# The second mixture of experts: seven single blocks spread between pair blocks

## The chip, the cores and the metric

The kernel runs on one core of a Trainium2 chip. The metric is the device time of one execution in microseconds (us). Below, TensorE is the matrix engine (PE in the profile), VectorE is DVE, ScalarE is ACT, GpSimd is POOL and SyncE is SP; SP only issues transfers here, and POOL issues the gathers and scatters by index.

## The reference

Two layers run one after the other over x of 4 x 1024 tokens with 256 numbers each. Each is x + mixer(norm(x)) * silu(ffn(norm(x))). The change touches only the expert part of the second layer:

```
gate_scores = jax.nn.softmax(x @ Wg + bg, axis=-1)
topk_scores, topk_idx = jax.lax.top_k(gate_scores, TOP_K)      # 2 of 8 experts
...
for e in range(NUM_EXPERTS):
    h = jax.nn.gelu(x @ W1[e] + b1[e])                         # 256 -> 1024
    y = h @ W2[e] + b2[e]                                      # 1024 -> 256
    output = output + y * combine_w[..., e:e + 1]
```

4096 tokens choose two experts each, so 8192 rows go through an expert. With the inputs used here the eight experts are chosen 1101, 1114, 920, 949, 1048, 972, 1104 and 984 times.

## The kernel before

The rows of the second expert part are gathered into blocks, and every block belongs to one expert. A **pair block** holds 256 rows (two tiles of 128), a **single block** holds 128. There are 32 pair blocks and 7 single blocks, 71 tiles in all. The routing on VectorE works out at run time which expert a block belongs to (`slot_expert`), which tokens its tiles gather (`token_of`) and to which rows of `result1` its output is scattered (`result_of`). With the counts above all 32 pair blocks hold rows, four of them in each expert, and four of the seven single blocks do; the last three single blocks are empty, and their scatters point past the end of the result and write nothing.

For the n-th block in order of processing (n from 0 to 38) the engines do this:

- SP loads the whole expert, 2180 KB, into one of three buffers, `WE[n % 3]` (line 2143). It may do so when block n-3 has left `WE`, that is when VectorE has taken the output of n-3 out of its bank (line 2142).
- POOL gathers the block's tiles into `xg` (line 1988, one indirect transfer for each tile).
- TensorE turns the rows (line 1078, "xg_turn"), multiplies them by W1 in eight column groups (line 1092, 32 matmul records of 256 columns for a pair block, 32 of 128 columns for a single one), and multiplies the result by W2 (line 1102, 32 records for a pair block, 16 for a single one). ScalarE copies the turned rows (line 1889) and does the gelu of each column group (line 1902). VectorE adds the bias and takes the output out of its bank (line 1651).
- POOL scatters the output, one indirect transfer for each tile (line 1999).

The order is written out once for all engines by `schedule1` (each engine walks the same list and does its own part). This is the loop, with the parts for the attention of layer 1 left out:

```
    for n in range(NSLOT):
        if n + 2 < NSLOT:
            add("load_rows1", n + 2)
        add("w1", n)
        if n + 1 < NSLOT:
            add("xg_turn", n + 1)
...
        add("w2", n)
...
        add("y1_out", n)
        if n + WR < NSLOT:
            add("load_weights", n + WR)
        if n == XS_AT:
            add("load_xs")
```

`WR` is 3 and `XS_AT` is 19. `load_xs` is 16 transfers of 512 KB each on SP (lines 2117 and 2118) that bring `x1` and the attention output `s1` back from memory for the final mix. They stand in SP's list behind the weights of block 22 and ahead of the weights of block 23, and SP issues in order. After the last block SP waits for all scatters and issues 16 loads of the results (line 2155, `both`); the final mix on ScalarE and VectorE and the stores (line 2158) follow.

`SLOT_TILES` gives each block's number of tiles in order of processing, and `SLOT_AT` its first tile in `token_of` and `result_of`. Before, `SLOT_TILES` is 32 twos and then 7 ones.

Of the kernel before, what the change touches and what calls it, by code (L numbers as in the profile page):

```python
# [24 lines left out]

E1, F1, TOPK = 8, 1024, 2
PAIR_SLOTS, SINGLE_SLOTS = T * TOPK // (2 * P), E1 - 1
SLOT_TILES = [2] * PAIR_SLOTS + [1] * SINGLE_SLOTS
SLOT_AT = [sum(SLOT_TILES[:n]) for n in range(len(SLOT_TILES))]
NSLOT = len(SLOT_TILES)  # L30
TILES1 = sum(SLOT_TILES)
SLOTS1 = TILES1 * P
# [10 lines left out]
def constants():  # L43
# [12 lines left out]
        ("row_no", np.tile(np.arange(P), (P, 1))),  # L56
        ("slot_start", np.tile(np.array(SLOT_AT) * P, (P, 1))),
    ]
# [440 lines left out]
def build(nc, a, out):  # L499
# [314 lines left out]
    def tensor(e):  # L814
        w = Waits(e)

        def fill_from(u):
            w.wait_ge(free[u.bank], u.before)

        def emptied(item):  # L820
            w.wait_ge(free[use[item].bank], use[item].emptied)
# [209 lines left out]
        for what, *at in plan1:  # L1031
# [38 lines left out]
            elif what == "xg_turn":  # L1070
                n, = at
                u = use["xg_turn", n]
                w.wait_ge(xg_in[n % XR], 16 * sum(SLOT_TILES[n % XR:n + 1:XR]))
                fill_from(u)
                out_v = PS[:, u.bank, :].rearrange("p (k n) -> p k n", k=KD)
                for j in range(SLOT_TILES[n]):
                    for k in range(KD):
                        m = e.transpose(out_v[:, k, j * P:(j + 1) * P], xg[:, n % XR, j, k * P:(k + 1) * P], ident)
                m.then_inc(full[u.bank], 1)
            elif what == "w1":  # L1080
                n, = at
                rows = SLOT_TILES[n] * P
                emptied(("xg_turn", n))
# [839 lines left out]
    def gpsimd(e):  # L1923
# [47 lines left out]
        for what, *at in plan1:  # L1971
# [6 lines left out]
            elif what == "load_rows1":  # L1978
# [7 lines left out]
                for j in range(SLOT_TILES[n]):  # L1986
                    tile = SLOT_AT[n] + j
                    e.indirect_dma_start(  # L1988
# [3 lines left out]
            elif what == "y1_out":  # L1992
# [4 lines left out]
                for j in range(SLOT_TILES[n]):  # L1997
                    tile = SLOT_AT[n] + j
                    e.indirect_dma_start(  # L1999
# [205 lines left out]
```

## Time and profile before

| | |
|---|---|
| median of 3 runs | 1260.48 us (1258.74 to 1261.28) |
| the profiled execution | 1254.79 us, of which span 1253.0 us |
| TensorE busy | 1097.0 us, 88% |
| VectorE, ScalarE, GpSimd busy | 52%, 43%, 29% |
| mean granted TensorE clock | 0.911 of full speed |
| expert blocks of layer 1 | 622 to 1205 us of the span |
| final mix and stores | 1208 to 1253 us |

Times inside the trace count from the start of the span. The profiled execution is 1.79 us longer than its span, and the median of the runs is 5.69 us above it. Busy shares are averages over stages with different limits; which engine sets the time of one stage is read from the waits in that stage.

### The profile page before, as it was taken

To read this page: it belongs to the slowest core of one execution; us is meant where nothing else is said; L and a number is where in the kernel's file an instruction comes from. 1 tells how busy PE (TensorE), PEld (TensorE's weight loads), DVE (VectorE), ACT (ScalarE), POOL (GpSimd) and SP (SyncE) were. 2 spreads that over 40 slices of the span, in tenths; PEclk is the share of its full clock that TensorE was granted. 3 is DMA by queue.
4 is the path that set the end of the run, shared out by engine and by line. 5 is a ranking of instruction groups with operands and counts; after the bars stand their busy time and mean duration, and the time that the engine had idled before them with its cause. 6 is when DMAs were issued, how large, how long until landed. Compare 5 with 4: busy or idle time off the path is not lost.

```text
span 1253.0 us, 16201 instructions
## 1 busy us (share of the span) xinstructions
PE 1097.0 (88%) x6006; PEld 958.5 (76%) x6006; DVE 645.6 (52%) x1330; ACT 539.3 (43%) x1133; POOL 368.1 (29%) x351
## 2 busy tenths in 40 slices
PE   3955699999999994999698999999999999999940
PEld 2933578888888883888587888888888888888940
DVE  6384477667677775646697656564710000000018
ACT  2212355455454445565545454554323332233445
POOL 1007144444444541000314323232223322222200
PEclk9677699999999997787598999999999999999975
DMA  9802402443343335426146434343555895455948
GB/s 294 239 8 102 151 1 84 133 127 100 113 126 119 113 113 182 166 83 256 72 152 244 148 143 156 134 170 118 194 191 193 288 395 185 177 185 198 337 154 269
DMA packets 100624, 207.07 MB, mean 165 GB/s; under 512 B 9819, under 2 KB 86119, under 8 KB 95553
## 3 DMA queue, kind: packets, MB, share of 16 engines
q1 hardware_dynamic: 88976, 174.70, 40.1%
q0 software_dynamic: 11568, 31.34, 7.6%
q8 instruction: 48, 0.79, 0.3%
q14 instruction: 32, 0.25, 0.1%
HBM read 159.08 MB, written 48.97 MB: 166 GB/s over the span
## 4 chain that ended last, share of the span: by engine, by line
PE 73%; DMA 5%; ACT 5%; issue 3%; SPq 3%; DVE 3%; POOL 1%; POOLq 0%; ACTq 0%
PE PS L1102 17%; PE PS L1092 16%; PE PS L843 7%; PE PS L994 5%; PE PS L933 4%; PE PS L882 4%; PE PS L1004 2%; PE PS L946 2%; PE PS L960 2%; PE PS L1054 2%; PE PS L891 2%; PE PS L971 2%; PE PS L832 1%; SPq L2117 1%; PE PS L1067 1%
## 5 line engine op out<-in xcount | busy, mean ns | idle before, releaser
L1092 PE MATMUL PS<-xgT,WE 128*128 128x256 f32 (+1 forms) x1248 | 259.6, 366 | 12.8 <-ACT xgT L1889 6.2
L1902 ACT ACTIVATE hT<-PS,WE 128x256 f32<-128x256 f32 (+1 forms) x312 | 139.9, 454 | 281.0 <-PE PS L1092 271.6
L1092 PEld LDWEIGHTS PS<-xgT,WE 128*128 128x128 f32 x1248 | 222.2, 193 | 43.5 <-ACT hT L1902 8.5
L1102 PE MATMUL PS<-WE,hT 128*128 128x256 f32 x1136 | 251.6, 379 | 0.0
L1102 PEld LDWEIGHTS PS<-WE,hT 128*128 128x128 f32 x1136 | 213.5, 190 | 27.8
L1651 DVE TENSOR_TENSOR y<-PS,WE 128x512 f32<-128x512 f32 (+1 forms) x39 | 25.1, 643 | 365.5 <-PE PS L1102 365.5
L1999 POOL DMA_INDIRECT result<-y,result_of x71 | 71.3, 1004 | 277.3 <-DVE y L1651 267.2
L1988 POOL DMA_INDIRECT xg<-xn_dram,token_of x71 | 73.6, 1037 | 152.8 <-DVE result_of L1567 131.4
L843 PE MATMUL PS<-XT,Wf 128*128 128x256 f32 x384 | 91.6, 397 | 0.0
L843 PEld LDWEIGHTS PS<-XT,Wf 128*128 128x128 f32 x384 | 76.4, 203 | 10.6
L1957 POOL TENSOR_TENSOR prob<-prob,row_sum 128x512 f32<-128x512 f32 x56 | 58.6, 1046 | 73.8 <-DVE row_sum L1307 73.4
L1950 POOL TENSOR_TENSOR sc<-sc,sc_max 128x512 f32<-128x512 f32 x56 | 58.4, 1043 | 71.8 <-DVE sc_max L1295 70.9
L933 PE MATMUL PS<-KB,Q 128*128 128x256 f32 x256 | 71.0, 403 | 7.2 <-DVE KB L1269 5.8
L994 PE MATMUL PS<-rowsT,wgu 128*128 128x160 f32 x512 | 75.6, 301 | 0.0
L994 PEld LDWEIGHTS PS<-rowsT,wgu 128*128 128x128 f32 x512 | 72.4, 190 | 2.6 <-issue 1.4
L832 PE MATMUL PS<-const,XN 128*128 128x128 f32 x128 | 32.0, 410 | 39.4 <-ACT XN L1840 19.2
L1976 POOL TENSOR_TENSOR MAG<-SQ 128x768 f32<-128x768 f32 x16 | 28.9, 1811 | 123.5 <-ACT SQ L1862 123.5
L882 PE MATMUL PS<-XT,qkv_w 128*128 128x256 f32 x256 | 63.0, 392 | 0.0
L832 PEld LDWEIGHTS PS<-const,XN 128*128 128x128 f32 x128 | 22.2, 206 | 46.8 <-ACT XN L1840 24.0
L1305 DVE TENSOR_REDUCE row_sum<-prob 128x8 f32<-128x512 f32 x64 | 43.6, 681 | 27.8 <-ACT prob L1781 23.7
L933 PEld LDWEIGHTS PS<-KB,Q 128*128 128x128 f32 x256 | 46.5, 202 | 13.4 <-DVE KB L1269 6.9
L882 PEld LDWEIGHTS PS<-XT,qkv_w 128*128 128x128 f32 x256 | 50.9, 199 | 7.5
(227 smaller groups left out, 1690.8 us busy)
## 6 DMA issues: line engine op xcount, KB each, us to landing
WE<-in_experts SPq DMA_DIRECT2D x39, 2180.0 KB
wgu<-in_w_gate SPq DMA_DIRECT2D x32, 256.0 KB, 2.7
wgu<-in_w_up SPq DMA_DIRECT2D x32, 256.0 KB, 3.1
wdn<-in_w_down SPq DMA_DIRECT2D x32, 256.0 KB, 3.4
both<-result SPq DMA_DIRECT2D x16, 512.0 KB, 8.7
table<-zeros POOLq DMA_DIRECT2D x1, 5160.0 KB, 29.5
rows<-table SPq DMA_DIRECT2D x32, 129.0 KB
X<-in_x SPq DMA_DIRECT2D x8, 512.0 KB, 9.5
```

The costliest lines, as they stand in the source:

```text
L832: m = e.transpose(out_v[:, k, j * P:(j + 1) * P], XN[:, 2 * pair + j, k * P:(k + 1) * P], ident)
L843: m = e.matmul(PS[:, u.bank, part * CH:(part + 1) * CH], Wf[:, n, k, part * P:(part + 1) * P], XT1[:, ch, k, :], start=k == 0, stop=k == K ...
L882: m = e.matmul(PS[:, u.bank, c * UT:(c + 1) * UT], qkv_w[:, k, col:col + P], XT0[:, unit, k, :], start=k == 0, stop=k == KD - 1)
L933: m = e.matmul(PS[:, u.bank, c * 256:(c + 1) * 256], Q2[:, unit % 2, c, win, :, :].rearrange("p e q -> p (e q)"), KB[:, c, win, :, :].rear ...
L994: m = e.matmul(PS[:, u.bank + f, n * CAP:(n + 1) * CAP], wgu0[:, ex % 2, n, k, f * P:(f + 1) * P], rowsT[:, grp % 2, k, j * CAP:(j + 1) * ...
L1092: m = e.matmul(PS[:, FIRST_H_BANK + nth % HR, 0:rows], W1[n % WR][:, k, c * P:(c + 1) * P], xgT[:, n % 2, k, 0:rows], start=k == 0, stop=k ...
L1102: m = e.matmul(PS[:, u.bank, j * D:(j + 1) * D], hT[:, n % 2, c, j * P:(j + 1) * P], W2[n % WR][:, c, :], start=c == 0, stop=c == KF - 1)
L1902: e.activation(hT[:, n % 2, c, 0:rows], PS[:, FIRST_H_BANK + (KF * n + c) % HR, 0:rows], ACT.Gelu_apprx_tanh, bias=b1[n % WR][:, c:c + 1], ...
L1950: e.tensor_tensor(by_head, by_head, sc_max[:, s % SR, :].unsqueeze(2).to_broadcast([P, PAIRS, WIN]), ALU.subtract).then_inc(sc_sub_done, 1)
L1957: e.tensor_tensor(prob[:, s % PR0, :, :], prob[:, s % PR0, :, :], row_sum[:, s % RR, :].unsqueeze(2).to_broadcast([P, PAIRS, WIN]), ALU.mu ...
L1988: e.indirect_dma_start(out=xg[:, n % XR, j, :], out_offset=None, in_=xn_dram, in_offset=bass.IndirectOffsetOnAxis(ap=token_of[:, tile:tile ...
L1999: e.indirect_dma_start(out=result1, out_offset=bass.IndirectOffsetOnAxis(ap=result_of[:, tile:tile + 1], axis=0), in_=y1[:, n % YR, j, :], ...
```

## The change

The seven single blocks no longer stand at the end of the list. The first is put at index 18, behind 18 pair blocks, and the others at 20, 22 and so on to 30, so that one pair block stands between two single ones. Eight pair blocks (31 to 38) follow the last single block. Each block keeps its tiles, its tokens and its expert; only the place in the order moves. Nothing is added or removed.

```
-SLOT_TILES = [2] * PAIR_SLOTS + [1] * SINGLE_SLOTS
-SLOT_AT = [sum(SLOT_TILES[:n]) for n in range(len(SLOT_TILES))]
+FIRST_SINGLE = 18
+BLOCKS = [(2, 2 * n) for n in range(PAIR_SLOTS)]
+for n in range(SINGLE_SLOTS):
+    BLOCKS.insert(FIRST_SINGLE + 2 * n, (1, 2 * PAIR_SLOTS + n))
+SLOT_TILES = [tiles for tiles, _ in BLOCKS]
+SLOT_AT = [at for _, at in BLOCKS]
```

Line numbers of the changed kernel are 4 higher. The first place is TensorE from the W2 product of block 19 to the W1 product of block 23. A row with `WE,hT` is W2, a row with `xgT,WE` is W1, a row with `const,xg` turns the rows of the next block. Before, all are pair blocks:

```order
L1102 MATMUL PS<-WE,hT 128x256 x16
L1092 MATMUL PS<-xgT,WE 128x256 x16
L1078 MATMUL PS<-const,xg 128x128 x4
L1102 MATMUL PS<-WE,hT 128x256 x16
L1092 MATMUL PS<-xgT,WE 128x256 x16
L1078 MATMUL PS<-const,xg 128x128 x4
L1102 MATMUL PS<-WE,hT 128x256 x16
L1092 MATMUL PS<-xgT,WE 128x256 x16
L1078 MATMUL PS<-const,xg 128x128 x4
L1102 MATMUL PS<-WE,hT 128x256 x16
L1092 MATMUL PS<-xgT,WE 128x256 x16
```

Now, at the same place of TensorE's list:

```order
L1106 MATMUL PS<-WE,hT 128x256 x16
L1096 MATMUL PS<-xgT,WE 128x128 x16
L1082 MATMUL PS<-const,xg 128x128 x4
L1106 MATMUL PS<-WE,hT 128x256 x8
L1096 MATMUL PS<-xgT,WE 128x256 x16
L1082 MATMUL PS<-const,xg 128x128 x2
L1106 MATMUL PS<-WE,hT 128x256 x16
L1096 MATMUL PS<-xgT,WE 128x128 x16
L1082 MATMUL PS<-const,xg 128x128 x4
L1106 MATMUL PS<-WE,hT 128x256 x8
L1096 MATMUL PS<-xgT,WE 128x256 x16
```

Blocks 20 and 22 have become single ones: W1 with 128 columns, and half as many W2 products. SP's list is the same in both kernels. This is its piece with the end of `load_xs` and the weights of block 23 (the changed kernel's lines):

```order
L2121 DMA xs_170<-x_dram 128x4x256
L2122 DMA xs_170<-s_dram 128x4x256
L2121 DMA xs_171<-x_dram 128x4x256
L2122 DMA xs_171<-s_dram 128x4x256
L2146 TENSOR_LOAD slot_expert
L2146 ISA x2
L2147 ISA
L2147 DMA WE<-in_experts 128x4360
```

Nothing moved there, so the sixteen `xs` transfers now stand beside smaller blocks. The third place is the end of POOL's list, where `result` rows are scatters and `xg` rows gathers. Before:

```order
L1999 DMA result<-y_163,result_of 8192x256
L1988 DMA xg<-xn_dram,token_of 128x256
L1999 DMA result<-y_163,result_of 8192x256
L1988 DMA xg<-xn_dram,token_of 128x256
L1999 DMA result<-y_163,result_of 8192x256 x3
```

Now:

```order
L2003 DMA result<-y_163,result_of 8192x256 x2
L1992 DMA xg<-xn_dram,token_of 128x256 x2
L2003 DMA result<-y_163,result_of 8192x256 x2
L1992 DMA xg<-xn_dram,token_of 128x256 x2
L2003 DMA result<-y_163,result_of 8192x256 x6
```

The last three blocks scatter two tiles each where they scattered one.

## Rows read from the trace of the kernel before

**Rows 1.** The page: the span, and busy time of the engines.

```profile
span 1253.0 us, 16201 instructions
PE 1097.0 (88%) x6006; PEld 958.5 (76%) x6006; DVE 645.6 (52%) x1330; ACT 539.3 (43%) x1133; POOL 368.1 (29%) x351
```

**Rows 2.** Chain that ended last, 974 to 1032 us: start, us, what.

```profile
974.13 6.92 PE PS L1102 x32
...
984.00 3.51 SPq L2117
...
1009.38 1.32 SPq L2118
...
1011.46 13.30 DMA WE<-in_experts
...
1024.89 7.14 PE PS L1092 x32
```

**Rows 3.** Timeline of PE, W1 of blocks 19, 20 and 23.

```profile
966.62 7.07 PE L1092 MATMUL PS<-xgT,WE 128*128 128x256 f32 x32
...
980.87 7.07 PE L1092 MATMUL PS<-xgT,WE 128*128 128x256 f32 x32
...
1024.89 5.42 PE L1092 MATMUL PS<-xgT,WE 128*128 128x256 f32 x24 [1.10 <-DMA WE<-in_experts]
```

**Rows 4.** Windows: busy by engine, granted clock, DMA share, GB/s at the end.

```profile
981.00:995.00 14.00, 14.00 (x69) 12.33 (x68) 0.69 (x1) 4.34 (x9) 4.05 (x4) 1.00 0.83 297
995.00:1009.00 14.00, 14.00 (x69) 12.32 (x68) 0.69 (x1) 4.35 (x9) 4.05 (x4) 1.00 1.09 354
1009.00:1024.00 15.00, 14.79 (x71) 12.69 (x69) 0.86 (x2) 4.34 (x9) 4.05 (x4) 1.00 1.08 395
...
1160.00:1168.00 8.00, 7.68 (x52) 7.05 (x52) 0.42 (x1) 3.32 (x9) 2.03 (x2) 1.00 0.94 353
...
1039.00:1053.00 14.00, 14.00 (x68) 12.34 (x67) 0.69 (x1) 4.35 (x9) 4.07 (x4) 1.00 0.52 193
```

**Rows 5.** DMA view of 1010 to 1015 us, then of 1020 to 1025 us.

```profile
DMA packets 1762, 1.74 MB, mean 349 GB/s; under 512 B 59, under 2 KB 1762, under 8 KB 1762
...
DMA packets 204, 2.12 MB, mean 424 GB/s; under 512 B 48, under 2 KB 48, under 8 KB 93
```

**Rows 6.** Timeline of the single blocks, 1160 to 1191 us.

```profile
1160.27 3.73 PE L1092 MATMUL PS<-xgT,WE 128*128 128x128 f32 x32
...
1162.97 1.03 POOL L1988 DMA_INDIRECT xg<-xn_dram,token_of  x1 [0.30 <-issue]
...
1171.87 0.20 PEld L1078 LDWEIGHTS PS<-const,xg 128*128 128x128 f32 x2 [0.28 <-DMA xg<-xn_dram,token_of]
...
1182.85 3.73 PE L1092 MATMUL PS<-xgT,WE 128*128 128x128 f32 x32
...
1190.10 3.73 PE L1092 MATMUL PS<-xgT,WE 128*128 128x128 f32 x32
```

**Rows 7.** PE behind two long waits (timeline), and a window behind the second.

```profile
622.27 10.07 PE L1092 MATMUL PS<-xgT,WE 128*128 128x256 f32 x32 [6.18 <-ACT xgT L1889]
...
678.32 6.77 PE L1092 MATMUL PS<-xgT,WE 128*128 128x256 f32 x20 [4.40 <-ACT hT L1902]
...
680.00:685.00 5.00, 5.00 (x18) 4.07 (x18) 4.93 (x10) 1.89 (x4) 0.80 (x1) 0.72 0.84 347
```

**Rows 8.** Timeline: output of a pair block, and of the last single one.

```profile
1153.22 0.69 DVE L1651 TENSOR_TENSOR y<-PS,WE 128x512 f32<-128x512 f32 x1 [13.34 <-PE PS L1102]
...
1155.99 0.97 POOL L1999 DMA_INDIRECT result<-y,result_of  x1 [0.30 <-issue]
...
1204.57 0.42 DVE L1651 TENSOR_TENSOR y<-PS,WE 128x256 f32<-128x256 f32 x1 [6.60 <-PE PS L1102]
```

**Rows 9.** Chain that ended last: last scatter of layer 0, last of layer 1.

```profile
478.37 2.17 DMA mixed_dram<-y,row_token
...
1205.77 2.10 DMA result<-y,result_of
```

## Prediction

> **What bounds the kernel now.** I read the page first. TensorE is busy 88% of a span of 1253.0 us [rows 1], so a change that moves only the order of its work matters where TensorE waits. Then I read the chain of waits over the expert blocks of the second layer. It is TensorE work almost without a break, with one exception: between 974 and 1025 us it leaves TensorE and runs through SP's issue of the `xs` transfers and then through the weights of block 23 [rows 2]. The reader should see three things there. The first `xs` transfers are issued at about 983 us and the last at 1009.38. The weights of block 23 (issued at 1011.46, landing 13.30 us later at 1024.76) come behind them. TensorE then waits for them, but only for 1.10 us [rows 3].
>
> The windows say why it is that long. From 981 to 1024 us the transfer engines are at shares of 0.83, 1.09 and 1.08, that is full, with 297, 354 and 395 GB/s, against 0.52 in the stretch of pair blocks behind it [rows 4]. The DMA view shows in what order the bytes move: from 1010 to 1015 us all 1762 packets are under 2 KB (the `xs` rows of 1 KB), from 1020 to 1025 us only 48 of 204 are [rows 5], the rest being expert weights. So the weights, issued at 1011.46, move behind the `xs` bytes and not beside them. This is a queue served in order, and the landing of block 23 is set by bytes and not by TensorE.
>
> The single blocks at the end, at a DMA share of 0.94 [rows 4], are near the transfer limit as well, but wait little. From W1 to W1 a single block takes 1190.10 - 1182.85 = 7.25 us; the three from 1160.27 to 1182.85 take 22.58, which is 0.83 above three times 7.25 [rows 6]. That 0.83 is late gathers.
>
> **The change part by part.** Sizes first. A pair block takes 980.87 - 966.62 = 14.25 us [rows 3], a single one 7.25 us [rows 6]. The number of both is unchanged, so the pure TensorE time is unchanged, and so is that of ScalarE, which does the gelu under it. What is left are waits.
>
> *The wait for the weights of block 23.* Call t0 the moment at which W2 of block 19 is done, 974.13 + 6.92 = 981.05 [rows 2]. Block 23's weights land at t0 + 43.7 and its W1 starts at t0 + 43.84 [rows 2]. Before, three pair blocks (20, 21, 22) stand between, 3 x 14.25 = 42.75, so the wait is 1.1. Now these are single, pair, single: 7.25 + 14.25 + 7.25 = 28.75. Does the landing come earlier with them? Its time is made of bytes: the weights of blocks 22 and 23 (2 x 2180 KB), 16 x 512 KB of `xs`, and the gathers and scatters of tiles of 128 KB. Before, three blocks bring 4 tiles each, so 12. Now the list gives scatter 19 (2 tiles), gather 22 (1), scatter 20 (1), gather 23 (2), scatter 21 (2), gather 24 (1), scatter 22 (1), gather 25 (2): again 12. The weights of block 22 are issued at t0 as before, the `xs` right behind; the weights of blocks 24 and 25 stand behind 23 in the queue. So I take the landing as unmoved, and the new wait is 43.84 - 28.75 = 15.1, which is **14.0 more than the 1.1 that it replaces**. Nothing hides it: the only later work that TensorE has is behind it in its own list. It would need a cover of 15 us, and both other buffers of `WE` have been used up. (The start of this stretch comes 7.0 earlier, block 18 being single, and behind it three more pair blocks and three fewer single ones are left, 3 x 7.0 = 21.0; the difference is the same 14.0.)
>
> The bounds of this term: all together are 12.85 MB and 12 x 0.131 MB, 14.4 MB, moved in about 42.4 us, 340 GB/s. At the 424 GB/s of the large packets [rows 5] they would take 34.0 us and the wait would be 6.7; at the 297 of the first window [rows 4], 48.5 and a wait of 21.2. I take the measured stretch itself, since the same bytes in the same order make it.
>
> The Trainium skill, "DMA: Bandwidth & Descriptors", section "Bandwidth", gives 425 GB/s for one 16 MB transfer into SBUF. By that figure the sum would be an estimate of some 9 us slower in place of the one below. The trace reaches it only with large packets; in the `xs` part it is 349.
>
> *Later weights.* Behind the wait, SP has already issued blocks 24 and 25 (their buffers are free from block 22's end at the latest), so they land under block 23. From then on single and pair alternate: a load is issued when block n is out and is needed two blocks later, 21.5 us. The run of single blocks shows loads that have only 14.5 us and cause no wait for `WE`. I cost this at nothing; the cover is one pair block, and without it the room is that of the single run.
>
> *The gathers.* The 0.83 us of late gathers goes away if a pair block lies between: **-0.83**. In the tightest new place, block 20, the gather of block 22 is issued some 4.3 us after W1 of block 20 begins and is needed 7.25 + 7.07 = 14.3 us after it. A gather issued at 1162.97 is waited for until 1171.87, 8.9 us at a DMA share of 0.94 [rows 6]. That leaves 1.1 us. At block 20 a miss costs nothing, the 15 us wait swallows it. At the five later places of this kind it would cost; I take 0, with a high end of 1 us each, 5.
>
> *The clock.* A wait of 15 us is new for TensorE in this stretch, where it has been granted 1.00. The two rows behind long waits show what comes next: after 6.18 us, the 32 records of W1 took 10.07 where they take 7.07, and after 4.40 us, 20 took 6.77 where they take 20/32 of 7.07, 4.4; in that stretch the granted clock is 0.72, a mix of the levels 1.2 and 2.4 GHz [rows 3, 7]. The costs are 3.0 and 2.4. I take the middle, **+2.7**; the low end is nothing (after the 1.1 us wait nothing was lost), the high end 3.0.
>
> *The end.* The last block is a pair block. VectorE's last step takes 0.69 in place of 0.42, and there is a second scatter, 0.97 + 0.30 [rows 8]: +1.54. The last scatter was of an empty block and ended 2.10 after its start; a scatter with rows, at the end of layer 0, took 2.17 [rows 9]. Together **+1.6**. The low end is 0.3, if the second scatter costs nothing; the high end puts the 8.9 of the loaded gather in place of 2.1, +8.4, which I think far off, since no weights move then.
>
> **Sum:** 14.0 - 0.8 + 2.7 + 1.6 = **+17.5 us**. Against the profiled execution, 1254.79, that is 1272.3; the median of the runs shown is 5.69 above that execution, so I forecast 1260.48 + 17.5 = **1278.0 us**.
>
> **The rivals.** *(A)* The forecast: the queue in order behind `xs`. For it: the 13.30 in the chain and the two kinds of packets [rows 2, 5]. Against: nothing in the trace; only the size is open.
>
> *(B)* Block 23's weights land in time. That needs them within 28.75 us of t0, so 14.4 MB at above 500 GB/s, or their passing the `xs` bytes. If it did, what remains is -0.8 + 1.6 = +0.8, at 1261.3, no difference. Against it: SP's issue itself is held until t0 + 30 by a full queue, its steps taking 1.32 to 3.51 us [rows 2].
>
> *(C)* The other side: the run of single blocks is transfer bound in the timed runs. Its share is 0.94 in the profile [rows 4], and the timed runs are 5.69 us longer than it. If all of that were weights arriving late in the run of single blocks, then spreading them gives it back: -5.7 - 0.8 + 1.6 = -4.9, at 1255.6. This decides only if B holds too, that is if the wait at block 23 stays under 5 us. Nothing in the profile shows a late `WE` in that run. The Trainium skill, "Perfetto Trace Analysis", section "Optimization Strategy", speaks for it: it says that regimes with different limits may gain from being interleaved, which is just what transfer-heavy single blocks among TensorE-bound pair blocks are. The trace gives this rule 0.83 us to win.
>
> *(D)* A, and the alternation brings late gathers in each single block: +5 on top, 1283.
>
> **How the numbers follow.** A has 80%, with a range of 1269 to 1285 (the wait between 6.7 and 21, drawn in towards the measured 15, and 2 us for the run-to-run spread of the medians); D has 9%, B 6%, C 5%. B and C together are 11%, so the range may leave them out and reaches into D: 1267 to 1286. A difference under 0.2% (2.5 us) can't be told from none. Faster by more: C, 5%. Within: B, 6%. Slower: A and D, 89%.
>
> **What would show it.** In the changed kernel's profile: one wait of TensorE at line 1096 for `WE` of 13 to 17 us, at about 1002 to 1018 us of the span, where the chain runs through SP's lines 2121 and 2122 and the weights; a granted clock under 1.00 in the 5 us behind it; no wait of TensorE for gathers between later single blocks, nor for weights; last scatter to first `both` load about the same, with the expert blocks ending 13 to 17 us later. The forecast is wrong if the weights of block 23 land earlier than t0 + 38 or the transfers' rate there differs by more than a tenth, if waits for `xg` appear in each single block, or if the last scatters take much longer than 2 us.

## The result and the profile after

The changed kernel takes 1275.58 us (median of 4 runs, 1272.84 to 1278.81) against 1260.88 us before (4 runs): a ratio of 1.012 with a 95% interval of 1.0092 to 1.0147, 14.7 us slower. The forecast was 1278.0 us, with a range of 1267 to 1286. Measured again on another chip, where both kernels are faster, it is 1245.41 against 1229.51, 1.0127 with an interval of 1.0103 to 1.0151, 15.9 us slower. Its profiled execution is 1275.98 us with a span of 1274.2 us, 21.2 us above the span of before.

First the page of the changed kernel: the span, and the slices of TensorE and of the granted clock.

```profile
span 1274.2 us, 16201 instructions
...
PE   4954699999999994999698999999999599999940
...
PEclk9667699999999996786598999999999889999975
```

There is one new hole in PE, the 5 in slice 32 (987 to 1019 us, 31.9 us a slice), and the clock's digits there and in the next slice are 8 where slices of full work have 9. The timeline of TensorE shows what it is, W1 of blocks 18, 20, 22 and 23:

```profile
954.98 3.73 PE L1096 MATMUL PS<-xgT,WE 128*128 128x128 f32 x32
...
976.48 3.73 PE L1096 MATMUL PS<-xgT,WE 128*128 128x128 f32 x32
...
997.98 3.73 PE L1096 MATMUL PS<-xgT,WE 128*128 128x128 f32 x32
...
1021.61 9.81 PE L1096 MATMUL PS<-xgT,WE 128*128 128x256 f32 x32 [16.01 <-DMA WE<-in_experts]
```

The last row answers to that of block 23 in [rows 3]: the wait for the expert's weights has gone from 1.10 to 16.01 us, and the 32 matmul records behind it take 9.81 us in place of 7.07. It is the only wait of TensorE between block 18 and the end; the kernel before had this one at 1.10 us and two of 0.3 us ahead of turns of gathered rows (at 1164 and 1171 us). The chain of waits takes the same way as before through SP [rows 2]:

```profile
969.73 6.92 PE PS L1106 x32
...
979.61 4.04 SPq L2121
...
1005.83 1.71 SPq L2122
...
1008.29 13.18 DMA WE<-in_experts
...
1021.61 9.81 PE PS L1096 x32
```

W2 of block 19 ends at 976.65. SP's issue of the `xs` transfers ends at 1007.5, 30.9 us later (29.7 before), the weights of block 23 move for 13.18 us (13.30), and W1 of block 23 begins 44.96 us after W2 of block 19 ended (43.84 before). The transfers kept their time to about 1 us, and TensorE came early. The windows of the changed kernel, with the granted clock third from the end, show the transfers full and the clock falling and coming back:

```profile
1001.65:1006.65 5.00, 3.95 (x21) 3.19 (x19) 0.42 (x1) 0.98 (x3) 1.36 (x2) 1.00 1.08 361
1006.65:1011.65 5.00, 0.00 (x0) 0.00 (x0) 0.00 (x0) 0.00 (x0) 3.04 (x3) 0.83 1.10 354
1011.65:1016.65 5.00, 0.00 (x0) 0.00 (x0) 0.00 (x0) 0.00 (x0) 0.00 (x0) 0.50 1.10 414
...
1021.65:1026.65 5.00, 5.00 (x12) 4.01 (x13) 0.00 (x0) 0.95 (x2) 0.00 (x0) 0.50 1.00 426
1026.65:1031.65 5.00, 5.00 (x24) 4.35 (x24) 0.00 (x0) 2.56 (x6) 0.00 (x0) 0.96 0.54 230
```

And the end, from the chain of the changed kernel, which answers to [rows 8, 9]:

```profile
1217.17 6.92 PE PS L1106 x32
1224.12 0.70 DVE y L1655
...
1225.59 0.97 POOL result L2003
1226.86 2.29 DMA result<-y,result_of
```

**Where the spans differ.** 21.2 us is more than the runs show, and part of it is not the change's. Block 18 is the first at which the kernels differ, and its W1 begins at 952.37 before and at 954.98 now, 2.6 later. From there to the end of the span it is 1253.0 - 952.37 = 300.6 us before and 1274.2 - 954.98 = 319.2 now, **18.6 us more**. I use this stretch for all traces below, since it leaves out what executions scatter ahead of block 18.

### The profile page after: what moved, and what is told of

It reads as the page before. It is cut to its first block, busy times and chain, and to the rows that moved or that the text cites. A ratio compares the mean times of both kernels' runs of the same rounds, so it can differ in the third digit from the quotient of the medians.

```text
span 1274.2 us, 16201 instructions
## 1 busy us (share of the span) xinstructions
PE 1100.7 (86%) x6006; PEld 963.4 (76%) x6006; DVE 645.4 (51%) x1330; ACT 539.0 (42%) x1133; POOL 368.0 (29%) x351
## 4 chain that ended last, share of the span: by engine, by line
PE 73%; ACT 5%; DMA 4%; DVE 3%; SPq 3%; issue 3%; another core or an unknown queue 2%; POOL 1%; POOLq 0%; ACTq 0%
PE PS L1106 18%; PE PS L1096 17%; PE PS L847 7%; PE PS L998 6%; PE PS L937 4%; PE PS L886 3%; PE PS L1008 2%; PE PS L964 2%; PE PS L1058 2%; PE PS L950 2%; PE PS L975 2%; PE PS L895 2%; PE PS L836 1%; SPq L2121 1%
## 5 line engine op out<-in xcount | busy, mean ns | idle before, releaser
L1096 PE MATMUL PS<-xgT,WE 128*128 128x256 f32 (+1 forms) x1248 | 262.3, 369 | 27.6 <-DMA WE<-in_experts 16.0
L836 PE MATMUL PS<-const,XN 128*128 128x128 f32 x128 | 31.9, 412 | 38.2 <-ACT XN L1844 18.9
L1980 POOL TENSOR_TENSOR MAG<-SQ 128x768 f32<-128x768 f32 x16 | 28.9, 1810 | 123.1 <-ACT SQ L1866 123.1
L950 PE MATMUL PS<-const,prob 128*128 128x128 f32 x256 | 40.9, 284 | 18.0 <-DVE prob L1314 10.0
```

Source lines behind the costliest of these rows:

```text
L836: m = e.transpose(out_v[:, k, j * P:(j + 1) * P], XN[:, 2 * pair + j, k * P:(k + 1) * P], ident)
L950: m = e.transpose(PS[:, u.bank, i * P:(i + 1) * P], prob[:, step % PR0, 2 * i:2 * i + 2, :].rearrange("p g k -> p (g k)"), ident)
L1096: m = e.matmul(PS[:, FIRST_H_BANK + nth % HR, 0:rows], W1[n % WR][:, k, c * P:(c + 1) * P], xgT[:, n % 2, k, 0:rows], start=k == 0, stop=k ...
```

## The experiments

The theory is that of the prediction: SP's queue is served in order, 8.4 MB of `xs` stand ahead of the weights of block 23, and single blocks give less TensorE work to cover them; the half-rate clock behind the wait and the second scatter at the end add to it. The rivals are that alternation costs by itself, that late gathers do, or that the wait is a matter of something else than bytes. In the edits shown, `...` marks lines left out. None of the kernels below leaves out work of the reference, and `filled` adds some that nobody reads.

**Stretch from W1 of block 18 to the end of the span, in us**

| kernel | W1 of 18 begins | span | stretch | expected | longest wait for WE |
|---|---|---|---|---|---|
| before | 952.37 | 1253.0 | 300.6 | | 1.1 |
| before, second profile | 958.37 | 1259.1 | 300.7 | 300.6 | 1.5 |
| changed | 954.98 | 1274.2 | 319.2 | | 16.0 |
| changed, second profile | 926.10 | 1245.3 | 319.2 | 319.2 | 16.2 |
| xs_last | 959.32 | 1259.6 | 300.3 | | none |
| singles_24 | 959.17 | 1260.2 | 301.0 | | 0.9 |
| old_xs31 | 957.71 | 1279.5 | 321.8 | | 19.1 |
| filled | 950.39 | 1266.6 | 316.2 | 316.3 | 1.2 behind 14.8 of work |
| xs_half | 950.40 | 1253.5 | 303.1 | 304 to 307 | 2.8 |
| empty_end | 948.59 | 1265.8 | 317.2 | 317.5 | 16.0 |
| covered | 948.85 | 1247.2 | 298.4 | 298.7 | none |
| covered, second profile | 927.52 | 1226.0 | 298.5 | 298.4 | none |

**xs_last: the new order, with the xs transfers behind all weights.**

```
-XS_AT = CHUNKS + 3
+XS_AT = NSLOT - 3
```

> The changed order, with load_xs moved from behind block 19 to behind block 36, where no weights are left to load. Theory A (the weights of block 23 queue behind the xs transfers): the 16.0 us wait of TensorE for WE is gone, the half-rate start behind it (2.9 us) too; the expert blocks end 18 to 19 us earlier than in the changed kernel, and two pair blocks (28.5 us) cover the xs transfers, so about 1258 to 1262 us, no difference from the kernel before (0.8 us of late gathers saved, 1.7 lost on the last scatters, 1.1 of the old wait saved). Rival 1 (alternating sizes or pair blocks at the end cost by themselves): most of the 15 us stays, over 1268. Rival 2: the xs transfers now delay the loads of the results, some 5 to 10 us come back, 1265 to 1270.

Measured: 1256.5 against 1258.0 us, ratio 0.9993 (0.9975 to 1.0011). TensorE does not wait once from block 18 on. Moving one entry of the list takes back 18.9 us, all of the 18.6 and 0.3 more, so the alternation and the pair blocks at the end together cost next to nothing (the terms below: 1.7 lost at the end against 0.8 of gathers and 1.1 of the old wait gained), and rival 1 falls. Rival 2 too: the last `xs` transfer is issued at 1194.94 and the first load of results at 1214.71, with the stretch at 300.3.

**singles_24: the xs transfers where they were, the single blocks six places later.**

```
-FIRST_SINGLE = 18
+FIRST_SINGLE = 24
```

> The single blocks at 24, 26 to 36 in place of 18, 20 to 30; load_xs stays behind block 19. So blocks 20 to 22 are pair blocks as in the kernel before, and only the alternation and the two pair blocks at the end are left of the change. Theory A: the wait for the weights of block 23 is 1 to 2 us as before, no loss of clock, 1259 to 1263 us. Rival 1 (the alternation or the end costs): over 1268 us. Rival D (late gathers in each single block): up to 5 us, 1264 to 1267, with TensorE waiting for xg.

Measured: 1259.0 against 1258.0 us, ratio 1.0014 (0.9994 to 1.0034), the wait for block 23 at 0.9 us. This is the same repair from the other side. Seven single blocks alternate with pair blocks here and TensorE waits for no gather, so the rival of late gathers, with 5 us, has no place.

**old_xs31: the old order, with the xs transfers at the single blocks.**

```
-XS_AT = CHUNKS + 3
+XS_AT = CHUNKS + 15
```

> The order before the change (single blocks last), with load_xs moved from behind block 19 to behind block 31, so that the three blocks ahead of the first delayed weights (35) are single ones. Theory A: weights of 35 land 44 us after the end of block 31, 3 x 7.25 = 21.75 us of work stand between, so a wait of about 22 us and 3 us of half-rate clock, less the 1.1 us wait at block 23; +24 us, about 1285 us. Rival 1 (what costs is the alternation, not the queue): no more than 5 us over the kernel before.

Measured: 1279.49 against 1258.0 us, ratio 1.0175 (1.0141 to 1.0209), and a stretch of 321.8, so 21.2 us more with no block moved, where 24 were expected. The timeline of its single blocks:

```profile
1170.29 0.44 PE L1078 MATMUL PS<-const,xg 128*128 128x128 f32 x2 [2.29 <-DMA xg<-xn_dram,token_of]
...
1200.57 5.45 PE L1092 MATMUL PS<-xgT,WE 128*128 128x128 f32 x32 [19.14 <-DMA WE<-in_experts]
```

W2 of block 31 ends at 1157.2, and W1 of block 35 begins 43.4 us later, where 44 was expected. The wait is split: 2.29 of it falls on a late gather between two single blocks under full transfers, the other 19.14 on the weights. Together that is 21.4 against the 22 expected. Behind it W1 of this single block takes 5.45 in place of 3.73, 1.7 more where 3 was expected; this is the largest part of the miss.

**before_again: the kernel before, a second profile.**

> The kernel before, unchanged, for a second profile. The two profiles so far start block 18 at 952.4 and 955.1 us though nothing ahead of it was changed, so 2.8 of the 21.2 us between their spans are not the change's. If that is scatter between executions, this profile starts block 18 somewhere in 951 to 957 us, waits 1 to 2 us for the weights of block 23, and the stretch from block 18 to the span's end repeats within 1 us (300.6).

Measured: W1 of block 18 begins at 958.37, six us later than in the first profile, and the stretch behind it is 300.7 against 300.6. The scatter of the spans lies ahead of block 18.

**filled: useless TensorE work in the wait.**

```
+                if n == XS_AT + 4:
+                    emptied(("inverse", CHUNKS - 1))
+                    for _ in range(34):
+                        e.matmul(PS[:, 7, 0:256], ident, const[:, 0:256], start=True, stop=True)
                 w.wait_ge(we_in[n % WR], 16 * (n // WR + 1))
```

> The changed kernel with 34 extra matrix products (128 x 256, into a bank of PSUM that nothing uses any more; nobody reads them) ahead of W1 of block 23, about 34 x 0.44 = 15.0 us of TensorE work in the 16.0 us wait. Nothing that the kernel computes is changed. If the 2.9 us by which W1 of block 23 is slow behind the wait are the clock, then its 32 records take 7 us again, and the stretch from W1 of block 18 to the span's end is 316.3 us in place of 319.2. Rival (W1 is slow because the weights are still landing, or for another reason tied to the transfers): it stays at 9.8 and the stretch at 319 us.

Measured: 1270.56 against 1253.16 us; the stretch is 316.2, 3.0 less than in the changed kernel. Its timeline of TensorE:

```profile
1000.85 14.84 PE L1091 MATMUL PS<-const 128*128 128x256 f32 x68
1016.91 7.17 PE L1100 MATMUL PS<-xgT,WE 128*128 128x256 f32 x32 [1.22 <-DMA WE<-in_experts]
```

W1 of block 23 takes 7.17 again. In the window where it runs, the granted clock is 1.00 while 24's and 25's weights move at 436 GB/s:

```profile
1016.00:1021.00 5.00, 4.09 (x19) 3.63 (x20) 0.00 (x0) 1.75 (x4) 0.00 (x0) 1.00 1.02 436
```

So the transfers alone do not slow W1. More work on TensorE made the stretch shorter. Of the 3.0 us, 2.6 are W1 of block 23 (9.81 against 7.17), and these are the clock. The changed kernel was not timed on the chip of this run, so the 3.0 rest on two traces.

**xs_half: half the bytes ahead of the weights.**

```
-        if n == XS_AT:
-            add("load_xs")
+        if n in (XS_AT, NSLOT - 3):
+            add("load_xs", int(n > XS_AT))
...
+            e.dma_start(xs[q][:, half, :, :], (x1_view, s1_view)[half][:, four, :]).then_inc(x_in[q], 16)
```

> The changed kernel with only the eight x1 transfers (4.19 MB) behind block 19, and the eight s1 transfers behind block 36. Theory A (bytes ahead in the queue set the landing): at 340 to 350 GB/s the weights of block 23 land 12.0 to 12.3 us earlier, the wait falls from 16.0 to about 3.8 us, and of the 2.9 us of clock none to all is left; stretch from block 18 to the end 304 to 307 us. Rival (a fixed cost of the weights' load, or the number of blocks ahead): the wait stays above 10 us.

Measured: 1255.3 against 1253.16 us, ratio 1.0031 (1.0018 to 1.0044). The timeline has

```profile
1003.82 7.15 PE L1096 MATMUL PS<-xgT,WE 128*128 128x256 f32 x32 [2.79 <-DMA WE<-in_experts]
```

The wait fell by 13.2 us for 4.19 MB, 317 GB/s, somewhat more than the 12.0 to 12.3 expected. After 2.79 us W1 takes 7.15, so none of the clock was lost, and the stretch of 303.1 is below the range that I gave. The wait follows the bytes; a fixed cost of the load, which would have left it above 10 us, is out.

**empty_end: an empty single block at the very end.**

```
-    BLOCKS.insert(FIRST_SINGLE + 2 * n, (1, 2 * PAIR_SLOTS + n))
+    BLOCKS.insert(FIRST_SINGLE + 2 * n if n < SINGLE_SLOTS - 1 else len(BLOCKS), (1, 2 * PAIR_SLOTS + n))
```

> The changed kernel with six single blocks at 18 to 28 and the seventh (an empty one) at the very end, as in the kernel before. The wait at block 23 is untouched. From the end of W2 of the last block to SP's first load of the results it was 3.5 us before and is 5.2 in the changed kernel. Theory (VectorE's larger step, one more scatter, and a scatter with rows): back to 3.5, stretch 317.5 us. Rival (the end is longer because pair blocks precede it): it stays at 5.

Measured: one execution, 1267.59 us; the stretch is 317.2, 2.0 less than in the changed kernel. Its chain at the end reads as in the kernel before:

```profile
1217.71 0.43 DVE y L1655
...
1218.91 2.10 DMA result<-y,result_of
```

From VectorE's step to the first load of results, at 1221.14, it is 3.4 us; in the changed kernel it is 5.2 (1224.12 to 1229.28). The rival falls, since pair blocks precede here too. No timed comparison stands behind this run.

**covered: what the theory calls best.** The order of empty_end, and

```
-XS_AT = CHUNKS + 3
+XS_AT = NSLOT - 4
```

> The version that the theory calls best: the order of the run empty_end, with load_xs behind block 35, when all weights have been issued; a pair, a pair and a single block (35.75 us) cover the xs transfers. No wait for weights (-1.1 against the kernel before), no late gathers in a run of single blocks (-0.8), the old end: stretch from block 18 to the end 298.7 us against 300.6, 0.15% faster than before, which timing alone may not tell from no change. Rival: late gathers or the xs transfers behind block 35 give it back, 300 us or more.

Measured: 1251.07 against 1253.16 us, ratio 0.9986 (0.9969 to 1.0004). The stretch is 298.4. The timed runs could not tell this from no change, so both were run again.

**after_again and covered_again.**

> The changed kernel again, for more timed runs and a second profile. By the traces it loses 18.6 us behind the start of block 18, by the first four timed runs 14.7 us over the whole. If the difference is scatter ahead of block 18, the stretch from block 18 to the span's end repeats as 319.2 within 1 us, with a wait of 16 us for the weights of block 23, and the ratio of the timed runs is 1.0148 (18.6 / 1258), above the 1.012 measured first.

Measured: 1.0127 (1.0103 to 1.0151), below the 1.0148 expected, which the interval holds; the stretch is 319.2 again, W1 of block 23 takes 9.86 us behind a wait of 16.2.

> The best version again. Its first trace has 298.35 us from block 18 to the end, 2.3 us less than the kernel before. If that holds, the stretch repeats within 0.5 us and the timed ratio is 0.998; the first measurement, 0.9986 with an interval of 0.9969 to 1.0004, could not tell it from 1.

Measured: 1226.26 against 1229.51 us, ratio 0.9975 (0.9962 to 0.9988), the stretch 298.5. This version is faster than the kernel before by 2.1 to 2.3 us in the traces and by 3 in these runs, and some 19 us faster than the changed one.

## Why the prediction was right

The time came out 2.4 us below the forecast, and the steps, taken one by one from the traces, are those that the prediction gave:

- **The wait at block 23**, forecast 14.0 more with a new wait of 15.1. Measured 16.0 less the 1.1 of before, 14.9 more. The step "I take the landing as unmoved" was off by 1.1 us against the first profile and by 0.7 against the second: W1 of block 23 begins 44.96 after the end of block 19 and not 43.84. It repeats. From W1 of block 20 to W1 of block 23 it is 45.1 in the changed kernel (976.48 to 1021.61) and in empty_end (970.09 to 1015.23), and 44.0 and 44.4 in the two profiles of before (980.87 to 1024.89, 986.88 to 1031.29). Up to the landing both move 15.4 MB, before at 352 GB/s and now at 343. That is 1.0 MB more than the 14.4 that the prediction added up: the next weights are issued right behind those of block 23 and before these land, which the sum left out; it weighs on both kernels alike. Most of the time is lost in one place. From 8.7 to 12.2 us behind the start of W1 of block 20 the transfers move 352 and 360 GB/s in the two profiles of before, 249 and 207 in the two of the changed kernel, 232 in empty_end and 228 in filled; some 120 GB/s less for 3.5 us are about 1.2 us, of which 0.3 comes back in the next 3. In this window POOL now issues the scatter of block 20 and both gathers of block 23 (985.34 to 989.00), and before it issued nothing. That these cause it is not shown.
- **That the queue and its bytes make the wait** is shown by five runs: without `xs` ahead no wait (xs_last), with pair blocks beside it 0.9 (singles_24), with single blocks beside it in the old order 21.4 (old_xs31), and with half the bytes 2.8 (xs_half). TensorE work put into the wait (filled) does not move the landing.
- **Later weights at nothing:** right. No wait for `WE` behind block 23 in any of these traces.
- **The gathers, -0.8:** right in size; the changed kernel has no wait of TensorE for a gather from block 18 on. In the narrow place, the gather of block 22 is issued at 980.77 and its rows are turned at 990.85 without a wait.
- **The clock, +2.7:** W1 of block 23 took 7.14 before, behind its own short wait [rows 2], and takes 9.81 now, 2.7 more; filled brings it back to 7.17. The granted clock fell from 1.00 to the lower level, 0.50, during the wait, and was up again some 5 us after work resumed. One of the two rows behind the forecast was weaker than it looked: ahead of the wait of 6.18 us TensorE had been granted 0.50 from 605 us on, so that row shows what a start at the lower level costs, 3.0, and not that the wait brought it. In the other the clock was 1.00 from 670 to 675 us and 0.59 from 675 to 680, and there the cost was 2.4.
- **The end, +1.6:** 1.74 from the end of W2 to the first load of results (5.19 against 3.45), and 2.0 by empty_end.

The terms as measured, 14.9 - 0.8 + 2.7 + 1.7 = 18.5, account for the 18.6 of the stretch to 0.1; forecast were 17.5, and 0.9 of the difference is the landing. The timed medians differ by 14.7 and 15.9, below both. The forecast's 17.5 lies inside both intervals (1.0139); the traces' 18.6 is 1.0148, just above the upper end of the first, and at 1.0151 of the faster chip at the upper end of the second. Each time only four runs of the changed kernel stand behind it, and two profiles of one kernel begin block 18 six us apart. Filled misses to the other side, 17.4 by the timed runs where the stretch differs by 15.6, so scatter ahead of block 18 is enough to explain such gaps; that it does so here is not shown. The forecast of 17.5 lies between the 18.6 of the traces and the 14.7 and 15.9 of the timed runs, and how near the time came to 1278.0 owes something to this scatter. Of the signs given in advance, one was out by the count used there: the expert blocks end 19.55 us later (1224.09 against 1204.54), not 13 to 17; counted from block 18 it is 16.9.

Of the rivals, (B) and (C), that the weights come in time, are refuted by the 16.0 us. (C) had taken the 5.69 us between the profiled execution and the median for late weights in the run of single blocks; before_again, on another chip, took 1260.97 us, as long as the median, with a stretch of 300.7 against 300.6, so those microseconds lie ahead of block 18. The interleaving rule of the Trainium skill, "Perfetto Trace Analysis", section "Optimization Strategy", had what I gave it: 0.8 us, and the trace agrees that it is a gain. covered takes it, without paying at block 23. (D), late gathers in each single block, is not seen in any alternating run; in old_xs31 one gather between two single blocks is late by 2.3.

## What to carry to other kernels

A large transfer without a deadline, issued on the queue that also carries the weights, takes its whole length out of the cover of the next weights (here some 29 us of issue for 8.4 MB); so where work is reordered, look first at what stands beside such a transfer, since shorter blocks there turn directly into a wait. Place it where the queue has nothing urgent left and the remaining work is longer than it. For comparing traces whose difference is small, count from the first instruction at which the kernels differ.

## What the runs showed of the hardware

- A wait of 2.8 us left TensorE's clock alone (xs_half, W1 7.15), one of 4.4 us cost 2.4 us [rows 7], and one of 16 us cost 2.7 us; with 14.8 us of products that nobody reads in that wait, W1 took 7.17 again.
- With weights alone (large packets) the transfers reached 436 GB/s beside W1 of a pair block at full clock (filled); while the 1 KB packets of `xs` moved, windows of 5 us show 347 to 366, apart from the dip named above.
- The two profiles on the faster chip differ from the others most in one place far ahead of the change. From 106 to 134 us, while POOL scatters the rows of layer 0, TensorE is busy 6.71 of 28 us in the changed kernel's first profile, VectorE and ScalarE only 4.65 and 1.97, and the profile names no cause. In its second profile TensorE is busy 24.35 us:

```profile
106.00:134.00 28.00, 6.71 (x33) 4.38 (x32) 4.65 (x9) 1.97 (x5) 18.04 (x19) 0.67 0.25 88
```

```profile
106.00:134.00 28.00, 24.35 (x153) 20.49 (x150) 18.93 (x36) 11.90 (x27) 21.27 (x21) 0.88 0.47 161
```

W1 of block 18 begins 28.9 us earlier there (926.10 against 954.98). That is more than this whole change, in kernels with the same instructions, and its cause stays open. The same stage explains most of the scatter of the other profiles: the product that ends the stall (`PS<-proj_w,OT`, L971 or L975) begins between 119.42 us (empty_end) and 137.95 us (xs_last) in the ten profiles on the slower chips, and block 18 begins between 948.59 and 959.32 us in the same order.
